# A one-block vision transformer with routed experts: a new order of the last steps on TensorE, VectorE, GpSimd and the store queue

## What is computed

```python
h = h + attention(layernorm(h))
flat = layernorm(h).reshape(S, 128)
h_shared = swiglu(flat @ shared_in_w.T)
out_shared = h_shared @ shared_out_w.T + shared_out_b
comb, cnt = route(flat)                  # (S, 8): weights and counts of the two chosen experts
h_expert = swiglu(flat @ expert_in_w.T)  # the same hidden rows for all experts
routed = cnt @ expert_out_bias
for e in range(8):
    routed = routed + comb[:, e:e+1] * (h_expert @ expert_out_weight[e].T)
h = h + out_shared + routed
```

## Time and profile before

| | |
|---|---|
| median of 3 runs | 464.65 us (463.91 to 466.17) |
| the profiled execution: device time | 468.48 us |
| its span, first to last instruction | 466.7 us |
| TensorE busy | 441.4 us (95%) |
| VectorE busy | 307.6 us (66%) |
| ScalarE busy | 190.3 us (41%) |
| GpSimd busy | 181.2 us (39%) |
| mean granted TensorE clock | 0.977 |

### The profile page before, as it was taken

One profiled execution on the slowest core, in us unless ns is written; L12 is line 12 of the kernel. 1 busy time (PEld: TensorE's weight loads), 2 busy tenths in 40 slices (PEclk: granted clock), 3 DMA queues, 4 the chain that ended last, 5 costly groups with the idle time before them and its releaser, 6 DMA issues.

```text
span 466.7 us, 6933 instructions
## 1 busy us (share of the span) xinstructions
PE 441.4 (95%) x2313; PEld 311.2 (67%) x2313; DVE 307.6 (66%) x896; ACT 190.3 (41%) x358; POOL 181.2 (39%) x220
## 2 busy tenths in 40 slices
PE   6969999899999999999999999999999999999982
PEld 2335455656786687667865788668856888887651
DVE  0151476486867876696659674868588877777665
ACT  1015523752276326641563238422752186321520
POOL 7112721222175306531652246304732256134453
PEclk9989999999999999999999999999999997899988
DMA  8998655135004520263007400530000000000000
GB/s 330 389 402 313 199 171 182 64 114 168 36 1 130 185 68 1 67 207 108 0 10 244 129 0 2 188 126 0 2 24 0 2 0 1 2 23 1 0 25 25
DMA packets 16451, 45.96 MB, mean 98 GB/s; under 512 B 1904, under 2 KB 7584, under 8 KB 16416
## 3 DMA queue, kind: packets, MB, share of 16 engines
q1 hardware_dynamic: 14704, 43.50, 27.8%
q10 hardware_dynamic: 1712, 2.02, 1.2%
HBM read 43.39 MB, written 2.13 MB: 98 GB/s over the span
## 4 chain that ended last, share of the span: by engine, by line
PE 77%; DVE 8%; DMA 4%; issue 4%; POOL 3%; ACT 2%; ACTq 1%; POOLq 0%; DVEq 0%
PE acc L483 22%; PE O L577 6%; PE B L469 6%; DMA bq_row<-in_bq_row 4%; PE scores L547 2%; PE scores L703 2%; PE C L703 2%; PE C L704 2%; PE C L705 2%; PE scores L705 2%; PE scores L704 2%; PE B L526 2%; PE C L635 2%; PE B L512 1%; PE C L665 1%
## 5 line engine op out<-in xcount | busy, mean ns | idle before, releaser
L483 PE MATMUL acc<-x_main,w_patch 128*128 128x512 f32 x288 | 141.4, 614 | 5.8 <-DMA w_patch<-in_w_patch 4.1
L483 PEld LDWEIGHTS acc<-x_main,w_patch 128*128 128x128 f32 x288 | 51.3, 195 | 48.3 <-issue 38.6
L1885 POOL TENSOR_TENSOR prod<-prod 128x512 f32<-128x512 f32 x31 | 39.9, 1286 | 27.9 <-DVE q_nat L1325 10.7
L993 ACT ACTIVATE probs_t<-B 128x512 f32<-128x512 f32 x32 | 19.1, 597 | 54.7 <-PE B L469 54.7
L577 PEld LDWEIGHTS O<-v_bd,probs_t 128*128 128x128 f32 x256 | 33.5, 200 | 10.4 <-issue 7.7
L1878 POOL TENSOR_TENSOR hidden_lo<-silu,hidden_hi 128x512 fp32r<-128x512 f32 x16 | 20.3, 1271 | 40.8 <-ACT hidden_hi L993 40.8
L577 PE MATMUL O<-v_bd,probs_t 128*128 128x64 f32 x256 | 33.2, 280 | 0.0
L1820 POOL TENSOR_TENSOR rstd<-var,neg_half 128x4 f32<-128x4 f32 x8 | 8.1, 1019 | 50.8 <-DVE var L1282 50.8
L1365 DVE TENSOR_TENSOR attn_patch<-O,row_rec 64x256 f32<-64x256 f32 x32 | 13.5, 422 | 21.5 <-PE O L577 20.8
L993 ACT ACTIVATE probs<-shift 128x512 f32<-128x512 f32 x32 | 20.1, 628 | 18.0 <-DVE shift L1338 16.8
L703 PE MATMUL scores<-w_eout_hi,hidden_hi 128*128 128x512 f32 x64 | 27.3, 426 | 0.0
(11 more groups left out here) (334 smaller groups left out, 1012.6 us busy)
## 6 DMA issues: line engine op xcount, KB each, us to landing
x_main<-in_x_main SPq DMA_DIRECT2D x40, 768.0 KB, 4.3
x_main<-in_x_main SPq DMA_DIRECT2D x8, 512.0 KB, 4.1
x_main<-in_x_main SPq DMA_DIRECT2D x8, 256.0 KB, 3.3
x_tail<-in_x_tail SPq DMA_DIRECT2D x8, 224.0 KB, 4.9
out_tokens<-y_out SPq DMA_DIRECT2D x14, 128.0 KB, 2.6
prod<-in_w_eout SPq DMA_DIRECT2D x2, 512.0 KB, 14.7
w_patch<-in_w_patch ACTq DMA_DIRECT2D x5, 192.0 KB, 10.1
silu<-in_w_in SPq DMA_DIRECT2D x2, 256.0 KB, 13.6
```

The costliest lines, as they stand in the source:

```text
L483: last = mm(acc[:, :], w_patch[:, j, :], x_main[:, j, :], start=(j == 0), stop=False)
L993: return nc.scalar.activation(dst, src, func, **kw)
L1885: q.tensor_tensor(p[r, 0, :], p[r, 0, :], p[r, 1, :], ALU.add).then_inc(tree1_done.sem, 1)
```

## The change

Six edits, all in the last stretch of the program. No instruction is added or taken away.

```diff
@@ SP @@
-            sp.wait_ge(ycls_done.sem, 1)
-            sp.dma_start(out[:, 0, :], y_cls[0:IMAGES, 0:D]).then_inc(stored.sem, 16)
-
...
             store_end(0, TILES - 1)
             need(sp, yout_done, GROUPS)
             store_end(TILES - 1, TILES)
+            sp.wait_ge(ycls_done.sem, 1)
+            sp.dma_start(out[:, 0, :], y_cls[0:IMAGES, 0:D]).then_inc(stored.sem, 16)
             sp.wait_ge(stored.sem, 32 * GROUPS + 32 + 16)
@@ TensorE @@
             counts(GROUPS, 1, IMAGES)
+            expert(L, 4, 128)
+            expert(L, 5, 128)
             shared_t(GROUPS, IMAGES)
-            expert(L, 4, 128)
             expert(GROUPS, 0, IMAGES)
             expert(GROUPS, 1, IMAGES)
             shared_natural(GROUPS, 1, IMAGES)
-            expert(L, 5, 128)
             expert(L, 6, 128)
             expert(L, 7, 128)
@@ VectorE @@
-            output(L - 1, TILES, 128)
             weigh(L, 1, 128)
             weigh(L, 2, 128)
             weigh(L, 3, 128)
+            output(L - 1, TILES, 128)
+            weigh(L, 4, 128)
             weights(GROUPS, 1, IMAGES)
-            weigh(L, 4, 128)
+            weigh(L, 5, 128)
             class_weigh()
-            weigh(L, 5, 128)
             shared_add(GROUPS, h2_cls, 1, IMAGES)
-            class_output()
-            output(L, TILES - 1, 128)
             weigh(L, 6, 128)
             last_tile(0)
             weigh(L, 7, 128)
+            output(L, TILES - 1, 128)
             last_tile(1)
+            class_output()
@@ GpSimd @@
             expert_sum(L, 1, 128)
+            expert_sum(L, 2, 128)
             class_sum()
-            expert_sum(L, 2, 128)
```

## The result

| | before | changed |
|---|---|---|
| median | 466.45 us (20 runs, 463.91 to 468.53) | 461.85 us (20 runs, 458.87 to 465.10) |
| ratio changed / before | | 0.9919 (0.9893 to 0.9945) |
| profiled execution, span | 466.7 us | 457.0 us |
| mean granted clock of it | 0.977 | 0.996 |
| count transpose of the class rows to the last addition | 19.00 us | 13.20 us |

The ratio makes 3.8 us less (2.6 to 5.0). It is that of the mean times, 466.09 and 462.33 us; the two medians lie 4.6 us apart. The two profiled spans differ by 9.7 us, and only about half of that is the change's: the other 4.7 (444.81 - 440.13) had come about before the first moved instruction, from where the clock fell in each execution. So I measure the change by the part of the trace that it touches, from the start of the class rows' count transpose (444.81 before, 440.13 after): it is 5.0 us shorter.

A forecast was written before the change was run, and what follows sets the result against it. Taken as bound: at the end, a TensorE gap, a slow clock behind it, and VectorE steps waiting for GpSimd. Last addition 5.3 us earlier less 0.57 for stores gives 4.7 off 464.65: 460.0 us, range 458.3 to 462.3.

The forecast's parts named there:

- TensorE: Two tiles moved ahead: gap gives 2.11 us, clock 1.57, less a tenth; last product ready 3.55 us earlier, at 454.4.
- rival B: TensorE's last products: clock falls again, or hadn't fallen there in the median run before; 461.5 us; chance 0.18.
- rival D: TensorE's clock falls at the moved products and stays low to the end: slower, 467.1 or 465.1 us; chance 0.02.
- The hold: VectorE additions of two SBUF operands wait for GpSimd's current addition: 1.4 us in the last tile, 0.5 in `weights(GROUPS)`.
- A: No hold in VectorE's last tile: last addition at 457.1, span saves 6.1 us, 458.6; chance 0.10.
- C: VectorE's last-tile additions all kept behind GpSimd until 457.0: last addition at 460.4, saves 2.8 us, 461.9; chance 0.08.
- the ceiling of the tail: Everything on VectorE from `last_tile(0)` waits until 457.0, then 0.68 us less than the whole tail follows: 460.4.
- The last addition: VectorE's last addition, holds included, ends at 458.5 in place of 463.81: 5.3 us earlier.
- The stores: Class store becomes a third issue behind the last addition: 0.57 us more, bounds 0.5 to 0.8; earlier stores don't delay it.
- The sum: Whole program: 5.3 - 0.57 = 4.7 us off the span, the same off the median of 464.65: 460.0; chance 0.62.

The follow-up runs named there:

- e3_filled: Kernel before with product 4's six matmuls made once more, without a signal, in TensorE's gap; end 20.30 us behind the count transpose, ratio to before 0.9962.
- e2_order_only: Changed kernel with TensorE's lines as before, so only VectorE, GpSimd and store orders changed; end 21.32 us behind the count transpose, ratio to before 0.9994.
- e4: Changed kernel with GpSimd's class sum left out; end 15.95 us behind the count transpose, ratio to the kernel before 0.9857.
- e6: Changed kernel with GpSimd summing the class rows ahead of tile 2 again; end 18.75 us behind the count transpose, ratio to the kernel before 0.9949.
- e9: Repeat of e5, one last-tile store on ScalarE's queue in the changed kernel; end 16.47 us behind the count transpose, ratio to the kernel before 0.9880.
- e1: Kernel before with only TensorE's order changed; end 19.46 us behind the count transpose, ratio to the kernel before 0.9957.
- e5: Changed kernel with one of the last tile's two stores issued from ScalarE's queue; end 16.47 us behind the count transpose, ratio to the kernel before 0.9874.
- e8: Changed kernel with the third addition of `last_tile(0)` moved behind the last weighing and `output(L, 3)`; end 16.57 us behind the count transpose, ratio to before 0.9863.
- e7: The changed kernel run again, unchanged; end 16.92 us behind the count transpose, ratio to the kernel before 0.9905.

## Why the prediction was right, and where it was not

**TensorE: right.** Forecast: the last product ready 9.6 us behind the transpose; measured 9.35. The gap gave 2.11 and the clock 1.58 (e3_filled) of the 1.57 forecast. The clock did stay up; rival B's first half, that the fall comes again, is refuted for this kernel: a gap of 2.11 us, with 64-column work beside it, was followed by a fall in all three profiles that had it. With it goes rival D. The rule that stood behind that rival, in the Trainium skill's page "TensorE: Matmul & The Clock Gate", section "HAM oscillation", puts the danger at longer gaps; the measurement decides against it here.

Rival B's second half was that the clock had not fallen there in the median run of before. Only three executions of such kernels were profiled, but the timed runs speak against it. Without this fall, and with as few others as the fastest run of the changed kernel (458.87), the kernel before would take some 458.87 + 5.0 - 1.58 = 462.3 us. The lowest of its 82 timed runs took 463.69, though 8 of 32 runs of the changed kernel came within 1.5 us of that kernel's lowest. So the fall came in all runs or nearly all.

**The hold: right in kind, and close in size for the last tile.** I took 1.4 us there; the rows give 0.14 + 0.94 + 0.25 = 1.33, and taking the class sum away gave 1.18. In `weights(GROUPS)` I added 0.5 to its 1.6 us, and it took 2.70 (443.50 to 446.20), 1.1 more: three of its steps took 0.45, 0.84 and 0.60 us where the same three take 0.15 to 0.16 in e2_order_only. That miss did no harm, since weighings follow each other 0.60 us apart and not 0.68 as I summed them: `weigh(L, 6)` started 8.01 us behind the transpose, forecast 8.3. Rivals A and C are out: the additions did not keep their old durations, and the tail ran on while GpSimd was still at work. Two small slips in the working did not carry into the forecast: tile 2's sum, 451.5 + 2.59, ends at 454.1 and not 454.3 (it took 2.73 under the holds, so 454.3 came true by luck), and the ceiling of the tail is 460.3 by its terms, not 460.4.

**The last addition: 5.8 us earlier, forecast 5.3.** 0.3 of the half microsecond is the earlier `weigh(L, 6)`, the rest is the tail behind it (448.14 to 453.33, 5.2 us, forecast 5.4).

**The stores: mis-sized.** "They don't delay it" was wrong. I let the first stores end at about the last addition; with `output(L, 3)` ending 1.24 us ahead of it the queue had four issues of some 0.63 us in line, so the class store came 1.38 us behind the last addition, not 1.14. The part behind the last addition took 3.68 us against 3.46, at the edge of the bounds; the end came 5.0 us earlier against 4.7. So this miss was more than made good by the last addition's half microsecond.

**The sum: the step that failed.** "I take the same 4.7 off the median: 464.65 - 4.7 = 460.0." What was right in the trace came out too low as a time, above all because I took three runs as the level of the kernel. Over 20 runs the kernel before has a median of 466.45, 1.8 more; less 4.7 that is 461.75, and the median measured was 461.85. That this median lies inside the range is no merit of the working: the range had the bounds of the holds and of the clock in the tail, and nothing for the level. Carried over by the ratio, the changed kernel would be at 460.9 where before is at 464.65, and at 462.7 where it is at 466.45, outside the range. Of those 2.7 us above the forecast, 1.8 are the level and 0.9 the gain, which the ratio puts at 3.8 and not 4.7.

The level moves because the clock falls elsewhere, and not at the same places in each execution. I had the rows for it, spoke of one place where there are two, and left it at "may differ from run to run". Of the changed kernel's 20 runs those with a mean clock of 0.996 or 0.993 took 458.87 to 459.60 us, those with 0.989 took 460.33 to 461.49, those with 0.986 took 461.73 to 461.93, and those with 0.983 or less took 462.94 to 465.10. In the twelve profiles the fall near 390 us lasted some 10.2 us in six executions (before and its copy, e2, e4, e6, e9), 3.4 us in four (e1, e3, e5, e8), and was missing in two, both of the changed kernel, one of which (e7) had a fall at 88 us instead. A second fall, of 3.4 us between 32 and 37 us, is in nine of the twelve and missing in the changed kernel's first profile, e1 and e3. Two pages show this for kernels with the same instructions up to the count transpose, e7 and e9:

```profile
PEclk9998999899999999999999999999999999999998
PEclk9989999999999999999999999999999999699999
```

A fall of 3.4 us shows as an 8 where most of it lies in one slice of 11.5 us, and as nothing where it is spread over two. The count transpose, up to which all these kernels run the same steps, started at 440.13 us in the profile with neither fall, at 440.60 and 440.97 with the short one near 390 alone, at 442.31 and 442.66 with that and the early one, and at 444.32 to 444.91 with the early one and the long one. Of the changed kernel's 32 timed runs the slowest (465.10) and the fastest (458.87) so differ by more than the whole gain.

**What stays open.** By the traces the gain is 5.0 us; the lowest runs of the two kernels, 463.69 and 458.87, say 4.8. The runs say 3.8 (2.6 to 5.0) and 4.4 (2.8 to 6.0). Both intervals reach 5.0, the first barely. Whether the changed kernel meets more falls earlier in the program, or had bad luck, these runs can't tell. Nor do they show why a fall comes at 32, 88 or 390 us in one execution and not in the next.

## What to carry to other kernels

Fill a wait of the bounding engine with work that is ready, even if that work is not urgent: here it gave back the gap (2.11 us) and the slow clock behind it (1.58). Edits on several engines have to be made together when each one's order assumes the other's: alone they gave 2.4 and 0.6 us, together 5.0. And before a forecast in absolute time, look at how far runs of one program lie apart and what their clocks are; here a level from three runs was off by 1.8 us, more than the forecast's terms for the holds (1.4), the clock (1.57) or the stores (0.57).

## What the runs showed of the hardware

A VectorE addition of two SBUF operands and a GpSimd addition keep each other waiting, in both directions: 128x128 took 0.29 us alone, 1.23 beside a GpSimd addition of 512 columns, and 1.71 where the end of a 128-column one went ahead of that, and GpSimd's 128-column addition took 0.65 in place of 0.45. Weighings that read PSUM stayed at 0.67 to 0.69. Moving the held addition bought next to nothing (0.15 us at the last addition). Six matmuls added to a gap of 2.11 us shortened the end of the program by 1.58 us. What I had not expected is that four stores issued back to back from one queue took some 0.63 us each, so that the queue and not the last result set when the final store started, 1.38 us behind it.
